# Summing softmax probabilities: one accumulator per block on GpSimd and VectorE in place of pairwise adds, and eight common PSUM banks

## What is computed

```
q = layernorm(x) @ wq                      # 8 heads of 128, in 2 groups of 4 heads
k, v = low-rank (32 latents a group), shared by the 4 heads of a group
scores = q k^T * scale, causal mask        # T = 1024
probs  = softmax(scores) = exp(scores - max) / sum(exp(scores - max))
y = probs @ v @ wo ;  x = x + layernorm(y)
# then: sigmoid router over 32 experts (6 of them kept), 16 anchor experts, 1 shared:
h = silu(x @ w_gate) * (x @ w_up), scaled by the router ;  out = h @ w_down
x = x + layernorm(out)
```

## Time and profile before

| | us |
|---|---|
| median of 3 executions | 415.49 (414.37 to 418.74) |
| the profiled execution | 416.28 |
| its span, first to last instruction | 414.2 |
| TensorE busy | 393.9 (95%) |
| VectorE busy | 281.5 (68%) |
| GpSimd busy | 275.7 (67%) |
| ScalarE busy | 231.4 (56%) |

### The profile page before, as it was taken

One profiled execution on the slowest core, in us unless ns is written; L12 is line 12 of the kernel. 1 busy time (PEld: TensorE's weight loads), 2 busy tenths in 40 slices (PEclk: granted clock), 3 DMA queues, 4 the chain that ended last, 5 costly groups with the idle time before them and its releaser, 6 DMA issues.

```text
span 414.2 us, 7003 instructions
## 1 busy us (share of the span) xinstructions
PE 393.9 (95%) x2168; PEld 260.5 (63%) x2168; DVE 281.5 (68%) x711; ACT 231.4 (56%) x450; POOL 275.7 (67%) x338
## 2 busy tenths in 40 slices
PE   8998999998999999999998999999999999999993
PEld 8664555553454644444556778767887788778871
DVE  5985897882857885526347776678765686557665
ACT  4555355564545466664675455865556655665643
POOL 6124867975976498473667886498963988477651
PEclk9989999998999999999999999999999999999997
DMA  7347090083230050500000000001000000000000
GB/s 215 52 108 169 16 220 13 0 196 52 40 38 3 2 77 3 71 9 2 3 0 2 1 1 2 0 0 28 1 1 2 25 2 0 1 2 25 0 2 25
DMA packets 9906, 14.56 MB, mean 35 GB/s; under 512 B 1232, under 2 KB 5520, under 8 KB 9488
## 3 DMA queue, kind: packets, MB, share of 16 engines
q1 hardware_dynamic: 9584, 13.49, 15.7%
q10 hardware_dynamic: 288, 0.64, 0.5%
HBM read 6.26 MB, written 1.05 MB: 18 GB/s over the span
## 4 chain that ended last, share of the span: by engine, by line
PE 77%; POOL 7%; DVE 6%; ACT 4%; issue 3%; DMA 2%; SPq 1%; POOLq 0%; DVEq 0%; ACTq 0%
PE ps L1240 9%; PE ps L1242 9%; PE ps L1241 9%; PE ps L1354 9%; PE ps L1333 9%; PE acc L1368 8%; PE total L1378 5%; PE acc L1439 4%; PE acc L1441 4%; PE acc L1440 4%; POOL silu L839 3%; DMA qst<-q_lo 2%; PE ps L1336 2%; PE ps L1356 1%; PE ps L1388 1%
## 5 line engine op out<-in xcount | busy, mean ns | idle before, releaser
L839 POOL TENSOR_TENSOR silu<-silu,cwb 128x512 f32<-128x512 f32 x80 | 102.5, 1292 | 40.3 <-ACT silu L971 35.8
L1095 DVE TENSOR_REDUCE nmax_h<-ps 128x1 f32<-128x512 f32 (+3 forms) x152 | 92.3, 655 | 47.8 <-PE ps L1336 24.3
L940 ACT ACTIVATE probs<-ps 128x512 f32<-128x512 f32 (+1 forms) x152 | 80.0, 579 | 70.2 <-PE ps L1354 43.7
L759 POOL TENSOR_TENSOR probs<-probs 128x768 f32<-128x768 f32 (+2 forms) x48 | 78.0, 1644 | 34.0 <-ACT probs L940 21.2
L1172 DVE TENSOR_TENSOR h_lo<-ps,h_hi 128x512 fp32r<-128x512 f32 (+1 forms) x84 | 57.0, 686 | 23.8 <-ACT h_hi L981 23.2
L1167 DVE TENSOR_TENSOR ps<-silu,ps 128x512 f32<-128x512 f32 (+1 forms) x84 | 57.9, 693 | 22.3 <-POOL silu L839 17.5
L971 ACT ACTIVATE silu<-ps 128x512 f32<-128x512 f32 x80 | 47.5, 597 | 45.5 <-PE ps L1242 39.7
L1333 PE MATMUL ps<-kst,qst 96*128 96x512 f32 (+3 forms) x192 | 63.8, 386 | 4.0 <-ACT probs L940 1.9
L1240 PE MATMUL ps<-xT_hi,w_hi 128*128 128x512 f32 x164 | 65.4, 399 | 1.3 <-ACT silu L971 1.3
L1242 PE MATMUL ps<-xT_hi,w_lo 128*128 128x512 f32 x164 | 64.4, 393 | 0.0
L1241 PE MATMUL ps<-xT_lo,w_hi 128*128 128x512 f32 x164 | 64.4, 393 | 0.0
(11 more groups left out here) (191 smaller groups left out, 518.7 us busy)
## 6 DMA issues: line engine op xcount, KB each, us to landing
qst<-q_hi SPq DMA_DIRECT2D x14, 256.0 KB, 5.6
qst<-q_lo SPq DMA_DIRECT2D x7, 256.0 KB, 6.1
x_sb<-in_attn_x SPq DMA_DIRECT2D x4, 256.0 KB, 6.5
raw<-in_ffn_w_gate SPq DMA_DIRECT2D x1, 1024.0 KB, 4.9
raw<-in_ffn_w_up SPq DMA_DIRECT2D x1, 1024.0 KB, 6.4
raw<-in_ffn_w_down SPq DMA_DIRECT2D x1, 1024.0 KB, 5.0
kst<-k_hi SPq DMA_DIRECT2D x6, 128.0 KB, 3.7
result<-x_sb SPq DMA_DIRECT2D x3, 256.0 KB, 2.3
```

What stands on the lines that cost most here:

```text
L759: nc.gpsimd.tensor_tensor(into, into, probs[:, k % KTBUF, js, cols], ALU.add).then_inc(added, 1)
L839: nc.gpsimd.tensor_tensor(silu[:, k % HRING, :], silu[:, k % HRING, :], cwb[:, m % 2, t // ET, :], ALU.mult).then_inc(scaled_ready, 1)
L940: nc.scalar.activation(probs[:, k % KTBUF, j:j + w, at:at + cols], bank(full)[:, 0:w * cols].rearrange("p (w c) -> p w c", w=w), ACT.Exp). ...
L1095: nc.vector.tensor_reduce(nmax_h[:, n % 2, i, j:j + w, h], bank(full)[:, 0:w * keys].rearrange("p (w k) -> p w k", w=w), AX.X, ALU.max, ne ...
```

## The change

The probabilities of a block are now all added into the buffer of its first tile. For tiles kt = 1 and on, GpSimd adds heads 0 to 2 in one instruction (part 0, three heads wide). Head 3 (part 1, SPLIT = 3) goes another way: ScalarE copies the first tile's head 3 into a PSUM bank ("seed"), VectorE adds each later tile to it there, and for the last tile ScalarE first copies the columns 0 to 383 back ("sum_copy") and VectorE writes the last sum to the buffer. Then one group of 4 ones matmuls of 512 columns serves the block. The buffers are handed out by `buffers()`: the first tile's is held until ones, the other three go round. All 8 banks are common: pv, ones, seed, down, the warm-up matmuls and the tail take theirs from the planner. In the expert part g of unit 0 no longer follows the last exp, and silu, hi and lo of the first three units wait only for the tile whose memory they lie over. The core of the diff:

```diff
-BANKS = 6
+BANKS = 8
 KTBUF = 4
+ADDERS = ("POOL", "DVE")
+SPLIT = (3,) * NB
...
+def buffers():
+    held, at, was = [None] * KTBUF, {}, {}
+    turn = list(range(KTBUF))
+    for n in range(NB):
+        for kt in range(kts(n)):
+            own = turn.pop(0)
+            if kt == 0:
+                first = own
+            else:
+                turn.append(own)
+            at[n, kt], was[n, kt], held[own] = own, held[own], (n, kt)
+        turn.append(first)
+    name = {at[NB - 1, kt]: k for k, kt in enumerate((1, 2, 3, 0))}
+    return {x: name[own] for x, own in at.items()}, was
...
-        step("DVE", ("nm_split", n), 45, n + 1, *[("max", *ev[1:]) for ev in steps], n >= 1 and ("shift", n - 1))
+        step("DVE", ("nm_split", n), 110, n + 1, *[("max", *ev[1:]) for ev in steps], n >= 1 and ("shift", n - 1))
...
-                step("PE", ("pv", n, kt), 10 + cols * 17 // 100, rank - 0.2, *exps, *vs,
-                     ("pv", n, kt - 1) if kt else n >= 1 and ("yl", n - 1))
-                if kt % 2:
-                    for half in range(2):
-                        step("POOL", ("add", n, kt, half), 2 * (8 + cols * 252 // 1000), rank - 0.1, ("pv", n, kt - 1),
-                             *[e for e in exps if half in halves_of(e)])
-                    step("PE", ("ones", n, kt - 1), 10 + (CH - first_col(n, kt - 1)) * 17 // 100, rank - 0.2, ("add", n, kt, 0), ("add", n, kt, 1),
-                     ("ones", n, kt - 3) if kt > 1 else n >= 1 and ("recip", n - 1))
-        step("DVE", ("recip", n), 170, n + 2, ("ones", n, kts(n) - 2))
+                step("PE", ("pv", n, kt), 10 + cols * 17 // 100, rank - 0.2, *exps, *vs, kt and ("pv", n, kt - 1),
+                     bank=0 if kt else 1, until=("yl", n))
+                if kt == 0 and SPLIT[n] < REP:
+                    step("ACT", ("seed", n), 22 + (REP - SPLIT[n]) * 41, rank - 0.1, *[e for e in exps if 1 in parts_of(e)], bank=REP - SPLIT[n], until=("add", n, kts(n) - 1, 1))
+                if kt:
+                    step("POOL", ("add", n, kt, 0), 18 + SPLIT[n] * cols * 215 // 1000, rank - 0.1, ("pv", n, 0),
+                         *[e for e in exps if 0 in parts_of(e)], kt > 1 and ("add", n, kt - 1, 0))
+                    step("DVE", ("add", n, kt, 1), 15 + (REP - SPLIT[n]) * cols * 105 // 1000, rank - 0.1, *[e for e in exps if 1 in parts_of(e)],
+                         ("add", n, kt - 1, 1) if kt > 1 else ("seed", n), kt == kts(n) - 1 and ("sum_copy", n))
+                if kt == kts(n) - 2:
+                    step("ACT", ("sum_copy", n), 22 + (REP - SPLIT[n]) * 31, rank - 0.1, ("add", n, kt, 1), ("pv", n, 0))
+        step("PE", ("ones", n), 10 + CH * 17 // 100, n + 2.9, *(("add", n, kts(n) - 1, part) for part in range(len(ADDERS))), bank=1, until=("recip", n))
+        step("DVE", ("recip", n), 170, n + 2, ("ones", n))
...
-        need = [("post_T_lo", m)] + ([("wsplit", 2, WSPLITS[-1]), last_exp] if k == 0 else [])
+        need = [("post_T_lo", m)] + ([("wsplit", 2, WSPLITS[-1])] if k == 0 else [])
...
-            step("ACT", ("silu", k), 60, rank, ("g", k), k >= HRING and ("h", k - HRING), k == 0 and ("ones", NB - 1, kts(NB - 1) - 2),
-                 1 <= k < HRING and ("silu", k - 1))
+            step("ACT", ("silu", k), 60, rank, ("g", k), k >= HRING and ("h", k - HRING), *(lies_over(k) if k < HRING else []))
...
+                elif kind == "add":    # VectorE
+                    ...
+                    into = probs[:, BUF[n, 0], j:end, cols] if last else late_sums(n)[:, :, cols]
+                    nc.vector.tensor_tensor(into, late_sums(n)[:, :, cols], probs[:, BUF[n, kt], j:end, cols], ALU.add).then_inc(added[part], 1)
...
-                    for j in range(REP):
-                        last = nc.tensor.matmul(total[LAT * j:LAT * j + LAT, cols], ones[:], probs[:, KT[n, kt] % KTBUF, j, cols],
-                                                start=(kt == 0), stop=(kt == kts(n) - 2))
+                    for j in range(REP):
+                        last = nc.tensor.matmul(bank(ev)[LAT * j:LAT * j + LAT, :], ones[:], probs[:, BUF[n, 0], j, :], start=True, stop=True)
```

More of the change, by code:

```diff
@@ L109, in p2_steps, with part_heads, parts_of @@
     return out
-def halves_of(ev):
-    return {j // 2 for j in range(ev[3], ev[3] + ev[4])}
+def part_heads(n, part):
+    return (SPLIT[n], REP) if part else (0, SPLIT[n])
+def parts_of(ev):
+    return {part for part in range(len(ADDERS)) if ev[3] < part_heads(ev[1], part)[1] and part_heads(ev[1], part)[0] < ev[3] + ev[4]}
+def buffers():
[12 more added lines that the diff above has]
+    return {x: name[own] for x, own in at.items()}, was
 WARM = 14
@@ L208, in chunk_of, with leaves @@
         return CPB * b + c
+    def leaves(user, parts=range(len(ADDERS))):
+        if user is None:
+            return []
+        n, kt = user
+        return [("pv", n, kt), *(("add", n, kt, part) for part in parts)] if kt else [("ones", n)]
     step("SP", ("x_load",), 320, 0)
@@ L215, in plan @@
     step("landing", ("late_in",), 500, 0.3)
-    step("PE", ("warm",), 560, 0)
+    step("PE", ("warm",), 560, 0, bank=1, until=("warm",))
     step("POOL", ("consts",), 220, 0)
@@ L234, in plan @@
     step("PE", ("xT", 0), 50, 1, ("xn_nrm", 0), ("xn_nrm0",), bank=1, until=("xT_lo", 0))
-    step("PE", ("hold",), 130, 0.5, ("xT", 0))
+    step("PE", ("hold",), 130, 0.5, ("xT", 0), bank=1, until=("hold",))
     step("ACT", ("xT_hi", 0), 60, 1, ("xT", 0))
@@ L300, in plan @@
             step("PE", ev, max(19, own * w * 23 // CH) + 25 * masked, rank, ("s_dma", n), b and ("unit_rows",), bank=1, until=("exp", *ev[1:]))
[L301 to L306, removed]
+            step("ACT", ("exp", *ev[1:]), 22 + w * own * 80 // 1000, rank, ev, *leaves(WAS[n, kt]))
@@ L383, in plan @@
         step("ACT", ("tail_copy", half), 38, rank, ("down", NU - 1), ("fin_T", NCH - 2), half and ("tail_copy", 0))
-        step("PE", ("tail_T", half), 27, rank, ("tail_copy", half), ("yl", NB - 1), bank=1 - half, until=("tail_center", half))
+        step("PE", ("tail_T", half), 27, rank, ("tail_copy", half), bank=1, until=("tail_center", half))
         step("DVE", ("tail_mom", half), 75, rank, ("tail_T", half), ("fin_mom", NCH - 2))
@@ L390, in plan @@
     return o, o.settle()
-KT_AT = [(n, kt) for n in range(NB) for kt in range(kts(n))]
-KT = {at: k for k, at in enumerate(KT_AT)}
+BUF, WAS = buffers()
 PLACED, PLAN = plan()
@@ L422 @@
 RSTD = count("POOL", "xn_rstd", "post_rstd", "post_rstd2", "fin_rstd")
-ADD = count("POOL", "add")
+ADD = [{ev: k + 1 for k, ev in enumerate(e for e in PLAN[engine] if e[0] == "add" and e[3] == part)} for part, engine in enumerate(ADDERS)]
 MUL = count("POOL", "mul")
@@ L541, in tiles, with sums, late_sums, rows_left @@
             return ap.rearrange("p (t d) -> p t d", d=D)
+        def sums(m):
+            return bank(("down", MT * m))
+        def late_sums(n):
+            return ps[:, BANK["seed", n]:BANK["seed", n] + REP - SPLIT[n], :]
+        def rows_left(engine, row):
+            kt = (1, 2, 3, 0)[row // REP]
+            engine.wait_ge(pv_done, PV["pv", NB - 1, kt])
+            for part in range(len(ADDERS)):
+                engine.wait_ge(added[part], ADD[part]["add", NB - 1, kt, part])
         def tail_tiles(half):
-            return tiles((total if half else bank(("tail_T", 0)))[:, 0:CH // 2])
+            return tiles(bank(("tail_T", half))[:, 0:CH // 2])
         def normed_of(ev):
@@ L592, in build @@
         pv_done = sem("pv_done")
-        added = sem("added")
+        added = [sem(f"added{part}") for part in range(len(ADDERS))]
         ones_done = sem("ones_done")
@@ L1327, in _ @@
                     pe.wait_ge(masks, 3)
[L1328 removed]
+                    bank_turn(pe, ev)
                     at = T * b + CH * h
```

237 lines of the change are left out of this document (132 added, 105 removed).

## The result

The changed kernel takes 414.16 us (median of 20 runs, 410.84 to 415.48), the kernel before 417.32 us beside it (20 runs, 414.03 to 426.35). The ratio is 0.9929, interval 0.9900 to 0.9958: 0.7% faster, where 2.1% were forecast. The profiled execution has a span of 412.0 us and takes 414.03 us. First the page after: busy time by engine, the slices, and the chain by engine.

The account below looks back on a forecast made before the run. TensorE was taken as the bound. Median 415.49 us, with long blocks going from 118 to 105.85 + I - M, less 2.3 (short blocks) and 1.4 (expert start), gave 399.6 + I - M = 406.6 us; range 400.5 to 418.5.

Parts of the forecast that it names:

- TensorE's saving: Ones matmuls: 20.6 us of groups become 8 groups of 512 columns, 8.0 us, saving 12.6 us at full price.
- GpSimd's work: Three-head additions on GpSimd, 3.48 us at the widest, add 20.6 us in all, 19.1 us of it in the long blocks.
- Where GpSimd decides: Long blocks 2 to 5, 118 us before: they take 105.85 us of GpSimd work plus its idle time less work moved out.
- I: GpSimd's idle time among the long blocks after the change, expected at 16 us, half of today's 31.25 us.
- M: GpSimd weight splits of the third matrix moved out of the long blocks, behind block 5: 9 of some 10.6 us.
- the prediction's signs: What the trace should show if right, including GpSimd above 85% busy among the long blocks and weight splits after them.
- VectorE's waits: VectorE additions waiting for an exp hold up maxima in the long blocks: between nothing and 10 us, taken as nothing.
- rival 3: TensorE waits longer and its clock falls, once more per other long block: 10 us, 416.8 us; chance 0.21 with other mixtures.
- The start of the expert part: First silu waits for tile 1's additions of the last block instead of the last ones group: 1.4 us gained.
- Rivals 2 and 4: GpSimd takes over as bound, 422.6 us, chance 0.11; expert matmuls too early hold banks, some 420 us, chance 0.05.

Follow-up runs that it names:

- a_nolock_warm: Changed kernel without VectorE's low-part subtraction, route comparisons formed on GpSimd, nine identity matmuls filling each of two transfer waits (blocks 1, 4): 405.84 us, ratio 0.9730.
- a_thin: Changed kernel with each GpSimd addition one head wide instead of three, the other two heads left out: 404.85 us, ratio 0.9731 to the kernel before.
- a_thin_warm: Changed kernel with GpSimd additions only one head wide and nine identity matmuls filling each of two transfer waits (blocks 1, 4): 400.17 us, ratio 0.9598.
- a_narrow: Changed kernel with each GpSimd addition issued as up to three instructions of one head, same sums: 417.52 us, ratio 1.0016 to the kernel before.
- a_nolock: Changed kernel without VectorE's low-part subtraction and with the route's two comparisons formed on GpSimd instead of VectorE: 410.78 us, ratio 0.9851 to the kernel before.
- a_order: Changed kernel with block 1's shift-row transfer issued ahead of block 3's first high-part queries again, as in the kernel before: 409.89 us, ratio 0.9816.
- a_warm: Changed kernel with nine identity matmuls ahead of block 1's first p2 and nine ahead of block 4's first p1, filling transfer waits: 408.69 us, ratio 0.9810.
- b_ones1: Kernel before, with ones groups of all pairs after a block's first cut to one column of one head, nothing in their place: 413.62 us, ratio 0.9917.
- a_nolow: Changed kernel without VectorE's subtraction that forms the low part of the row minimum, which stays zero: 412.49 us, ratio 0.9888 to the kernel before.

## Why the prediction was wrong

**TensorE's saving** (12.6 us): right in the prices (8 groups of 1.00 us). That it is worth its full price did not hold. Together with the 1.4 us of the start of the expert part 14.0 us were to be had; 3.2 us came, and even at equal clock 7 to 9.9 us by the medians and 8 to 10 us in the traces' balance.

**GpSimd's work** (+20.6 us): right, 3473 ns against 3.48 us, and 297.3 - 275.7 = 21.6 us in all by the pages.

**Where GpSimd decides** (I = 16, M = 9): In the same 118 us (72 to 190) GpSimd is idle 118 - 102.3 = 15.7 us, as I was set, but M failed. The last split of the third weight matrix starts at 137.35 us, 11 us later than before, still among the long blocks. With M = 0 the same sum gives 415.6 us, close to what was measured (0.9929 of 415.49 is 412.5), but that is not the cause: a_nolock_warm has 4 us more work on GpSimd and the same order, and takes 0.9730 of the kernel before. GpSimd is 102.3 / 118 = 87% busy there, and the prediction's signs, "above 85%", held, but "weight splits after them" did not. GpSimd's price is real but smaller: 5.7 us at equal clock by a_thin, locks included, and 1.3 points between a_nolock_warm (0.9730) and a_thin_warm (0.9598).

**VectorE's waits** ("I take nothing"): the first failed step. The wait that the prediction had in mind, an addition that waits for its exp and holds up the maxima, is small: VectorE stood idle some 6 us ahead of all its additions from 72 to 213 us, and TensorE's waits for maxima there are 1.7 us. What it left out was the lock. The prediction applied the exclusion rule of the Trainium skill ("SBUF — State Buffer", section "Who interferes with whom": a VectorE instruction with two SBUF inputs and a GpSimd one that reads SBUF keep each other out) to the new additions only, found them free, and looked for large rows. The trace agrees with the rule where it was not looked for: rows of 0.2 us that had always been there lasted up to 3.25 us, where up to 213 us the longest had been 0.47 us. That the change made GpSimd's additions longer (2.38 to 3.47 us) is the cause by a_narrow, where the excess of the same rows shrank with them from 10.9 to some 5 us; that they also stand closer together (87% busy) was not tested alone. It is worth 0.8 points (a_nolock), with the reserve of its interval.

**The clock** (rival 3; it and every other mixture within 1% had a share of 0.21): the second failed step, and the one that took most of the gain. The forecast's sum has no term for it: it held TensorE's clock at that of the kernel before. Three falls of 3.4, 3.4 and 5.1 us stand against two of 1.7 us. Rival 3 had the mechanism and too small a price (1.7 us for the gap and 1.7 for the fall; the falls measured two to three times that, on top of gaps of about 2.1 us), and its place wrong: not one event for each long block and not exps, but a 16 KB transfer that the new order put behind 512 KB (a_order: 1.1 points), a transfer wait of block 4 that was there before (2.12 us, 1.66 before), and VectorE's lock. At block 4 the rows name "issue" and an exp, but in both kernels the last k transfer fits: issued at 89.66 and landing in 7.3 us, against 89.74 and 7.9 us before, so at 97.0 and 97.6, with the product 0.2 us behind each. The transfers start as before; TensorE, with less work, arrives 1.2 us sooner. The prediction also read one fall of the kernel before and missed the one at 20 us, which has no long gap ahead of it. No step of the prediction read SP's queue for what the new order passes, and none asked which existing gaps would grow. a_warm and a_nolock_warm show it: with two places filled and the locks gone the ratio is 0.973, a larger gain than the forecast's 0.979, without a shorter wait for GpSimd (2.0 us at the ones groups, 1.8 in the kernel after).

**b_ones1** shows that the premise of the prediction, "a matmul taken off TensorE is worth its full price", was too strong in itself: 12.6 us less work gave 3.5 us, and 6.9 us at equal clock.

**The start of the expert part** (-1.4 us): TensorE's two gaps there are gone, but the last addition ends at 218.9 us, not near 209 as predicted, and the last ones group starts at 220.07 us, 1.5 us later than before. Rivals 2 and 4 did not come: GpSimd was late, not the bound; the first g or u row is at 213.84 us (213.00 before), and silu's table was loaded once.

## What to carry to other kernels

When work is taken off an engine whose clock depends on its being fed, list the gaps that it already has and price each at gap plus fall; the removed work was also what filled them. Filling such a gap with identity matmuls shows what the fall alone costs. When one engine's instructions get longer, look for every small instruction that excludes them, not only for the new ones. When an order is planned anew, compare the transfer queue's order line by line: one small transfer issued behind a large one cost 1.1% here.

## What the runs showed of the hardware

- From 12 to 232 us the traces of the 14 kernels have 18 gaps of 2.05 to 4.75 us on TensorE. With 17 of them the granted clock fell to 0.50, its lower level (1.2 GHz against 2.4), during the gap or within 2.3 us of its end. The exception is a_nolow: a gap of 2.10 us at 97.13 us with the clock at 1.00 on both sides, where the kernel after fell at the same product (below). Of 11 gaps of 1.16 to 1.81 us with the clock at 1.00 ahead of them, 5 came with a fall and 6 did not. Each fall cost 1.7 to 5.1 us.

```profile
97.13 0.48 PE L1417 MATMUL ps<-kst,qst 96*128 96x512 f32 x1 [2.10 <-issue]
```

```profile
90.00:97.00 7.00, 5.03 (x31) 2.90 (x31) 3.52 (x8) 3.33 (x7) 6.52 (x7) 1.00 0.87 112
97.00:106.00 9.00, 8.86 (x60) 5.08 (x61) 7.24 (x13) 6.56 (x14) 8.42 (x9) 1.00 0.01 3
```

- A fall needs no such gap: seven of the traces have one of 1.7 us at 20 to 32 us (the kernel before at 20.4) with no gap above 0.6 us since 12 us. What else decides was not found.
- A GpSimd addition of two SBUF inputs stays on one line up to 1536 elements: 1.00, 2.64 and 3.47 us for 384, 1152 and 1536.
- One kernel's 43 runs, on one core each of three chips, spread over 411.1 to 421.0 us of span, mostly with the granted clock.
